# Two depthwise convolutions: gathering conv 2's rows through a DRAM scratch, with every load and store of x issued by SyncE

## The reference

```python
x = x + conv(gn(x), k1)      # 3x3, padding 1, one filter per channel
w = (w + rot90(w) + rot180(w) + rot270(w)) * 0.25
x = x + conv(gn(x), w)       # 7x7, padding 3, one filter per channel
# gn: 32 groups of 12 channels, mean and variance over (12, 128, 128) of one image
```

## Time and profile before

| | |
|---|---|
| median of 3 runs | 3548.77 us (3547.64 to 3551.12) |
| the profiled execution's own time | 3551.22 us |
| its span in the profile | 3549.4 us |
| TensorE matmul busy | 83% |
| TensorE weight load busy | 47% |
| VectorE, ScalarE, GpSimd busy | 64%, 61%, 44% |
| DMA, mean of the whole span | 241 GB/s |
| mean granted clock of TensorE | 0.923 of full |

### The profile page before, as it was taken

The page is one execution under the profiler, slowest core; times in us unless marked ns, Lnnn a source line. Parts: engine busy times, 40 slices in busy tenths (PEclk is TensorE's granted clock), DMA queues, the critical chain, the costliest instruction groups (busy, mean ns, idle before and its releaser), DMA issues.

```text
span 3549.4 us, 86790 instructions
## 1 busy us (share of the span) xinstructions
PE 2933.2 (83%) x28676; PEld 1667.2 (47%) x28676; DVE 2254.7 (64%) x4988; ACT 2173.1 (61%) x3969; POOL 1565.6 (44%) x1552
## 2 busy tenths in 40 slices
PE   0568888879888889888888888888988888988896
PEld 0235544445454445544445444444544544544453
DVE  3546656666666666666667666666666666666663
ACT  1446656566566666666567666666666656666672
POOL 3324444444444444444445445444444435444452
PEclk9789999999999999999989899999998999999998
DMA  7798888878888888888888888888888988888887
GB/s 132 184 243 250 247 244 243 251 224 251 247 247 247 243 249 243 250 248 250 245 246 250 244 239 252 249 246 245 252 244 235 258 235 257 246 248 249 251 238 202
DMA packets 1081258, 853.90 MB, mean 241 GB/s; under 512 B 204344, under 2 KB 990776, under 8 KB 1080664
## 3 DMA queue, kind: packets, MB, share of 16 engines
q1 hardware_dynamic: 675224, 646.03, 65.5%
q10 hardware_dynamic: 405504, 201.38, 20.0%
HBM read 262.32 MB, written 221.88 MB: 136 GB/s over the span
## 4 chain that ended last, share of the span: by engine, by line
PE 53%; SPq 22%; issue 14%; DMA 5%; POOL 3%; DVE 3%; ACT 0%; ACTq 0%; POOLq 0%; DVEq 0%
PE PS L718 27%; PE PS L690 24%; SPq L230 16%; DMA BT<-H 4%; SPq L239 4%; POOL H L611 3%; SPq L258 2%; PE PS L655 0%; DVE X L364 0%; PE PS L662 0%; DMA rows<-v_all 0%; ACTq L542 0%; ACT TMP L546 0%; DVE TMP L418 0%; DVE H L457 0%
## 5 line engine op out<-in xcount | busy, mean ns | idle before, releaser
L718 PE MATMUL PS<-BT,BAND 126*32 126x512 f16 x21504 | 1343.6, 411 | 439.7 <-issue 333.2
L690 PE MATMUL PS<-H,BAND 128*128 128x512 f16 x6912 | 1574.0, 387 | 115.2 <-issue 56.5
L619 POOL TENSOR_TENSOR H<-Z,H 128x512 f16<-128x512 f32 x768 | 865.7, 1130 | 1289.1 <-ACT Z L531 1270.2
L718 PEld LDWEIGHTS PS<-BT,BAND 126*32 126x32 f16 x21504 | 785.9, 133 | 992.1 <-issue 553.8
L690 PEld LDWEIGHTS PS<-H,BAND 128*128 128x128 f16 x6912 | 860.2, 127 | 777.9 <-issue 133.6
L611 POOL TENSOR_SCALAR H<-X,RB 128x512 f16<-128x512 f32 x768 | 674.7, 893 | 652.2 <-DVE RB L424 416.8
L528 ACT ACTIVATE H<-X,RB 128x512 f16<-128x512 f32 x768 | 618.3, 805 | 219.6 <-DVE H L457 214.7
L511 ACT ACTIVATE Z<-X,RB 128x512 f32<-128x512 f32 x768 | 561.4, 802 | 104.1 <-DVE RB L424 91.9
L531 ACT ACTIVATE Z<-X,RB 128x512 f32<-128x512 f32 x768 | 615.1, 801 | 0.0
L554 ACT ACTIVATE DUMP<-X 128x512 bf16<-128x512 f32 x768 | 476.3, 621 | 158.6 <-DVE X L484 158.4
L435 DVE SCALAR_TENSOR_TENSOR X<-PS,SC,X 128x2048 f32<-128x2048 f32 x192 | 451.4, 2351 | 188.7 <-PE PS L718 177.0
(11 more groups left out here) (45 smaller groups left out, 359.6 us busy)
## 6 DMA issues: line engine op xcount, KB each, us to landing
BT<-H SPq DMA_DIRECT2D x1152, 174.6 KB
X<-in_x SPq DMA_DIRECT2D x768, 256.0 KB, 4.0
out_y<-X ACTq DMA_DIRECT2D x768, 256.0 KB, 4.8
BT<-H SPq DMA_DIRECT2D x1152, 149.6 KB
BAND<-rows SPq DMA_DIRECT2D x96, 220.5 KB
rows<-v_all SPq DMA_DIRECT2D x8, 1764.0 KB, 11.8
BAND<-rows SPq DMA_DIRECT2D x192, 51.0 KB, 2.9
BAND<-rows SPq DMA_DIRECT2D x192, 49.5 KB, 3.1
```

Of the source, the lines that this page charges most:

```text
L619: g.tensor_tensor(part(H1, n, 1, img, O1, P1), Z[:, img, :].rearrange("p (c w) -> p c w", c=CC), part(H1, n, 0, img, O1, P1), ALU.subtract ...
L690: last = mm(PA[:, ch, :], band[:, j, ws, :], data[:, :, O1 - 1 + j:O1 - 1 + j + W], start=k == 0, stop=k == 3 * K1 - 1)
L718: last = mm(banks2(n)[b * BL:(b + 1) * BL, ch, :], band[:, j, :], rows, start=j == 0, stop=j == K2 - 1, tile_position=(0, b * BL))
```

## The change

SyncE first writes the high and the low terms of a chunk to a scratch in DRAM (`stage`, two DMAs of 128 rows), and gathers from there: one DMA per term, which carries all four blocks of 42 rows. The scratch has five rows of zeros above and below, written once at the start, so that all blocks have 42 rows and BT needs no memset. In a step SyncE now issues bands, the two stage DMAs, the load of chunk t+6, the three gather DMAs and last the store of chunk t-5, which ScalarE issued before. GpSimd's next high parts wait for the two stage DMAs of two chunks before, no longer for the gather.

```diff
-LANDED = 16 * TERMS * NB
+LANDED = 16 * TERMS
+ROWS = P + 2 * HALO
...
+    staged = nc.dram_tensor("staged", (2, 2, ROWS, CC * L2), F16, kind="Internal").ap()
...
+            def stage(n, which, done):
+                q = n % 2
+                sp.dma_start(staged[q, which, HALO:HALO + P, :],
+                             H2[:, q, which, :, :].rearrange("p c l -> p (c l)")).then_inc(done[q], 16)
...
             def gather(n, k):
                 q, which = n % 2, (0, 1, 0)[k]
-                for b in (0, 2, 1, 3):
-                    lo_row, hi_row, r0 = window(b)
-                    first = TERMS * r0 + k
-                    sp.dma_start(BT[first:first + TERMS * (hi_row - lo_row - 1) + 1:TERMS, q, b, :, :],
-                                 H2[lo_row:hi_row, q, which, :, :]).then_inc(gathered[q], 16)
+                rows = staged[q, which, 0:WIN, :]
+                rows = bass.AP(rows.tensor, rows.offset, [[CC * L2, WIN], [BL * CC * L2, NB], [1, CC * L2]])
+                sp.dma_start(BT[k:KW:TERMS, q, :, :, :].rearrange("p b c l -> p b (c l)"),
+                             rows).then_inc(gathered[q], 16)
...
+            def store(n, at):
+                c, half = n % CPU_, (n // CPU_) % HALVES
+                ch0 = (at(n - n % GCH) // GCH) * GC + c * CC
+                wait_apart(sp, out_done, at(n) + 1)
+                for img in range(NI):
+                    dst = out[half * NI + img, bass.ds(ch0, CC), :, :].rearrange("c h w -> h c w")
+                    sp.dma_start(dst, xs(n, img)).then_inc(stored[n % BODY], 16)
...
+                n = t - 3
+                if real(n):
+                    q, turn = n % 2, (at(n) - n % 2) // 2
+                    if n >= 2:
+                        wait_apart(sp, gathered[q], turn * LANDED)
+                    else:
+                        sp.wait_ge(halo_zeroed, 64)
+                    wait_apart(sp, hi_done[1], NI * at(n) + NI)
+                    stage(n, 0, high_staged)
+                    wait_apart(sp, lo_done[1], NI * at(n) + NI)
+                    stage(n, 1, low_staged)
+
                 n = t + AHEAD            # the load: as before, with its wait on stored
...
                 n = t - 3
                 if real(n):
-                    if n < 2:
-                        sp.wait_ge(blocks_zeroed, 1)
-                    else:
+                    if n >= 2:
                         wait_apart(sp, conv2_done, at(n) - 1)
-                    wait_apart(sp, hi_done[1], NI * at(n) + NI)
+                    wait_apart(sp, high_staged[q], turn * 16 + 16)
                     gather(n, 0)
                     gather(n, 2)
-                    wait_apart(sp, lo_done[1], NI * at(n) + NI)
+                    wait_apart(sp, low_staged[q], turn * 16 + 16)
                     gather(n, 1)
+                if real(t - 5):
+                    store(t - 5, at)
...
 # ScalarE: its store of chunk t-5 is gone
 # GpSimd, ahead of the high parts of chunk n:
-                    wait_apart(pool, gathered[n % 2], ((at(n) - n % 2) // 2) * LANDED)
+                    wait_apart(pool, high_staged[n % 2], ((at(n) - n % 2) // 2) * 16)
+                    wait_apart(pool, low_staged[n % 2], ((at(n) - n % 2) // 2) * 16)
...
-                    g.memset(flat32(BT[:]), 0.0).then_inc(blocks_zeroed, 1)
```

More of the change, by code:

```diff
@@ L33 @@
 HALO = 5
-EDGE = 36
 TERMS = 3
 KW = TERMS * WIN
-LANDED = 16 * TERMS * NB
+LANDED = 16 * TERMS
+ROWS = P + 2 * HALO
 CUT = 4
@@ L127, in conv_program @@
         vectors_stored = [sem("vectors_stored1"), sem("vectors_stored2")]
-        blocks_zeroed = sem("blocks_zeroed")
         passed = sem("passed")
@@ L132, in conv_program @@
         stored = [sem(f"stored{r}") for r in range(BODY)]
+        high_staged = [sem(f"high_staged{q}") for q in range(2)]
+        low_staged = [sem(f"low_staged{q}") for q in range(2)]
+        halo_zeroed = sem("halo_zeroed")
         gathered = [sem(f"gathered{q}") for q in range(2)]
@@ L313, in _ @@
             cut1(1, G)
+            sp.wait_ge(zeroed, 10)
+            for rows in (slice(0, HALO), slice(HALO + P, ROWS)):
+                for q in range(2):
+                    sp.dma_start(staged[q, :, rows, :].rearrange("s r l -> r s l"),
+                                 H2[0:HALO].rearrange("p a s c l -> p (a s c l)")[:, 0:2 * CC * L2]
+                                 .rearrange("p (s l) -> p s l", s=2)).then_inc(halo_zeroed, 16)
             walk(sp, slot)
@@ L533, in normalise1 @@
                                      scale=rb[:, 0, img:img + 1]).then_inc(normed[0], 1)
[L535 to L542, removed]
             def take_root(layer, u):
@@ L571, in slot @@
                     act.wait_ge(fin[0], (at(n) // CPU_) * FIN + FIN)
[L572 to L576, removed]
+                if real(n):
+                    for img in range(NI):
+                        normalise1(n, img, at)
                 if real(t):
@@ L607, in high_parts2 @@
                 if n >= 2:
-                    wait_apart(pool, gathered[n % 2], ((at(n) - n % 2) // 2) * LANDED)
+                    wait_apart(pool, high_staged[n % 2], ((at(n) - n % 2) // 2) * 16)
+                    wait_apart(pool, low_staged[n % 2], ((at(n) - n % 2) // 2) * 16)
+                if n == 0:
+                    pool.wait_ge(halo_zeroed, 64)
                 rb = RB[:, 1, (n // CPU_) % 2]
@@ L626, in slot @@
                     low_parts1(t + 1, at)
-                if t == 1:
-                    pool.wait_ge(vectors_stored[1], 16)
-                    g.memset(flat32(BT[:]), 0.0).then_inc(blocks_zeroed, 1)
             walk(pool, slot)
```

## The result

| | us |
|---|---|
| after, median of 4 runs | 4036.73 (4023.4 to 4045.76) |
| before, beside them | 3548.20 (3543.14 to 3551.12) |
| ratio | 1.1376, 95% interval 1.1347 to 1.1405 |
| forecast | 3714, range 3440 to 4080 |

A forecast was written before the change was run, and what follows sets the result against it. SyncE's issuing was taken as the bound, with the DMA engines nearly full and next to bind. 188.4 us plus 191 steps of 18.45 us gave 3712, plus 1.8 made 3714 us; range 3440 to 4080.

The forecast's parts named there:

- SyncE issues without a pause, and is the bound: Kernel before: SyncE's queue issues DMAs continuously and everybody else waits for its end, 17.60 us a step.
- SyncE ceases to be the bound: After the change SyncE needs 12.2 us of issues a step with bands, against 16.3 to 17 before.
- 760 rows instead of 468: Rows moved per step: 504 gathered plus 256 staged, against 468 gathered before.
- The price of a row, 0.187 us: DMA engines' time per 4256-byte row, from the fastest stretch read, 339 GB/s; the kernel before's mean was 0.228.
- A fill of 0.95: Expected mean share of the 16 DMA engines, against 0.87 before; 280 engine-us then give 18.45 us a step.
- the new wait: SyncE's load of chunk t+6 waits for the store of chunk t-6: 0 in the sum, 3 us a step if uncovered.
- The rule weighed: A DMA uses the most engines up to 16 dividing its outermost sizes: 14 for 42 rows, 18.4 us; even spread 17.5.
- rows keep their price: Rival: each of 760 rows costs 0.228 us, 20.5 us a step, 4106 us; chance 0.10.
- The loads starve: Rival: loads wait behind stores in one queue, 20.0 us a step with half the steps hit, 4010 us; chance 0.16.
- The longer way: From high parts to conv 2 through DRAM: 17 to 18 us instead of 14 to 16, hidden, 3 us a step otherwise.
- The faster rival: SyncE was the only bound; at a fill of 1.03 the step is 17.0 us, 3437 us; chance 0.27.
- SyncE's issues, 12.2 us a step with bands: SyncE's summed issue time per step after the change: 4.1 + 1.4 + 2.1 + 2.5 + 2.1, the stores taken at 2.1.

The follow-up runs named there:

- Term-major order: Scratch gather with ScalarE's stores, each term sent to 42 neighbouring partitions of BT instead of every third, bands loaded to match: 4440.86 us, against 3856 without that edit.
- the wide gather: Changed kernel with ScalarE's stores and scratch rows laid out so one gather DMA of 128 partitions replaces three of 42: 3553.60 us, 0.9995 of the kernel before.

## Why the prediction was right or wrong

- *SyncE issues without a pause, and is the bound: wrong in the second half.* The rows were read rightly, the cause was not. With four issues less almost nothing moved (0.9973); with half the bytes in the gather the time fell 6.6%, and only then were the four issues worth 152 us. The DMA engines' work bounded the kernel before, and SyncE came close behind, held by them for part of its time. The rows had the sign of it: gathers that take 0.71 us at the least averaged 0.82 to 0.88, with the share at 0.87. Hence "SyncE ceases to be the bound" earned nothing.
- *760 rows instead of 468: right*, 145,992 packets.
- *The price of a row, 0.187 us: the failed term.* The mechanism was right (more rows than before, so more work for the DMA engines), its size was not. It came from one stretch of two microseconds, "made of large packets". It was 0.220, near the upper bound of 0.228 that the prediction kept as a rival. 760 x 0.033 = 25 engine-us, of which 20 show in the sum (300 against 280, the other packets being a little cheaper): at a share of 0.95 that is 1.3 us a step, 250 us. The reason that I gave, that a stage DMA "walks all 128 partitions evenly", holds for the stage (0.16 us a row, the estimate above) and not for the gather, whose 42 partitions in steps of three cost at least as much from DRAM, by that estimate (760 x 0.220 - 256 x 0.16) / 504 = 0.25 us, as from SBUF.
- *A fill of 0.95: 0.93*, 0.4 us a step, 80 us. The two terms together are 1.71 x 191 = 327 us, the whole miss. That 0.95 came so near is partly luck. The sum put the new wait at 0 and the one queue at nothing, and the same transfers with the stores on ScalarE's queue fill the engines to 1.00, in a kernel that is 181 us faster. So the price of the rows isn't the only step that failed: what the store's move costs was in no term of the sum, and the fill hid it.
- *The rule weighed.* Its 14 engines for 42 rows stood as one of two readings, with 18.4 us. One gather DMA with 126 partitions took 480 us longer than with 128. By the rule on the number of engines (the Trainium skill, DMA: Bandwidth & Descriptors, "Why a DMA increments its semaphore by 16 and not by 1") the first runs on 14 engines and the second on 16. The time moves in the sense of that rule. It doesn't show it by itself, since the number of engines and the partitions that each stands on changed together. Term-major order, with 42 rows to a gather DMA as before, shows that the partitions matter too: 585 us.
- *The rival "rows keep their price"*, 4106 us, had the best price of a row and a chance of 0.10; its time is 69 us too long. *"The loads starve"*, 4010 us with 0.16, was the nearest in time, by luck: it took the rows at 0.187 and 296 us for the wait. The wait exists, and the landing of stores has 24% of the chain, but taking it off the chain gave 60 us net of the 181 that the store's move costs. The other 120 were not in any case: with all transfers in one queue the mean share stayed under 1, with two it reached 1.00 and 1.05.
- *The longer way: rightly put at 0 here.* The landings of stage and gather have 2% of the chain each. It was hidden behind the stores, and shows once they are gone (34% with the stores on ScalarE).
- *The faster rival (0.27)* rested on the bound read wrongly. The fill of 1.03 that it needed is reached, but as a mean only by the wide gather with two queues.
- *SyncE's issues, 12.2 us a step with bands*: the gather's part was right (2.58 us for three), the stores took 7.19 instead of 2.1. SyncE was not relieved: its queue has 50% of the chain, and in the two steps shown above, where gaps were to be the sign of relief, the longest is 0.6 us.
- *Two slips in the sums.* 280 / (16 x 0.95) is 18.42, not 18.45, which is 5 us. The four chances add up to 0.98, and "faster 0.27" is the whole of the faster rival, with nothing taken off for the 0.05 of no change.

## What to carry to other kernels

An engine that always issues may be held by what it feeds: compare the mean of its issues with their least, and look at the DMA share before calling it the bound. Price a moved row from the mean of rows that go the same way, and where only a short fast stretch speaks for less, keep the mean as the forecast. How a DMA's rows fall on the partitions decides as much as their number: with one gather DMA over all 128 partitions, and loads and stores on two queues, a path with 41% more bytes (1204 against 854 MB) was as fast as the direct one.

## What the runs showed of the hardware

- The same bytes in the same number of packets cost 0.228 or 0.291 us a row, depending on whether 42 rows go to every third or to neighbouring partitions.
- One DMA of 126 partitions instead of 128, of four rows each, took the kernel from 3554 to 4033 us.
- With loads and stores on separate queues the DMA share was higher in both pairs of kernels: 1.00 against 0.93, 1.05 against 0.99. The second queue also had its own issuing engine, and why the two fill the DMA engines better than one was not taken apart.
- An issue on SyncE has no fixed length: a store's took 0.372 us at the least, 0.997 in the median and 6.467 at the most in the changed kernel.
- The mean share and the share of short stretches are different things: with one queue a stretch of 2 us reached 1.21, and the mean stayed at 0.93.
- 352 GB/s over 2700 us is the highest rate that any of these kernels held; the kernel before holds 246.
